# A decoder layer on one core: expert rows that carry their weight and result address, finished tiles scattered to token order, a longer tile pipeline, and blocks 0-1 and 2-3 as groups

## The chip, the cores and the metric

The kernel runs on one core of a Trainium2 chip. The metric is device time in microseconds (us) of one execution, lower is better. The chip has a tensor engine (PE, its weight loads PEld), a vector engine (DVE), a scalar engine (ACT), GpSimd (POOL) and a sync engine (SP) that in this kernel issues all plain DMAs. POOL issues the indirect ones.

## The reference

Input `x` is 2 x 1024 x 256 float32. One layer computes, on every token:

```python
x = layernorm(x + causal_linear_attention(x))          # 16 heads, 128 random features
x = layernorm(x + differential_cross_attention(ctx, x)) # 32 half-heads, 77 context rows
scores = sigmoid(x @ gate_w.T)                          # 16 experts in 4 groups
topk_idx = top 4 of the experts in the best 2 groups    # by scores + e_bias
topk_weight = 2.5 * scores[topk_idx] / sum(scores[topk_idx])
y = sum over the 4 experts of weight * (silu(x Wg) * (x Wu)) Wd   # 256 -> 128 -> 256
x = layernorm(x + y + shared_expert(x))
```

So each of the 2048 tokens has 4 expert rows, 8192 rows in all. The expert of a row is known only at run time.

## The kernel before

The tokens are cut into 4 blocks of 512 (`TB`), two for each batch element. `schedule()` writes out one list of jobs, (kind, block or group, number), and every engine walks the same list in order and does its own part of each job. An engine that waits in a job does not go on to the next one. Semaphores (`signal`) tie the parts together.

**Attention steps.** `attention_jobs(t)` gives the linear-attention work of one head per step, 64 heads' steps for 4 blocks plus 4 to drain. Jobs of the previous block's *chain* are merged between them.

**The chain of a block**, `chain_jobs(b, s)`: s=4 output projection and first norm, s=5 queries, s=7 to 9 cross-attention scores, s=10 maxima, s=11 to 15 24 `probs` chunks and 16 `weigh` jobs and the second norm, s=16 transposes, s=17 to 19 gate, routing (`route` 0 to 3 on DVE) and shared expert, and `prefix`, in which `slots(b)` makes the address of each expert row. At s=20 `dispatch` lets POOL write the rows with 16 indirect DMAs into the DRAM tensor `rows_in` of the block's group, sorted by expert, `keep` stores the residual sums, and after the last block of a group `ends` lets SP write 16 zero tiles behind the experts' last rows. In each `probs` chunk ACT makes two exponentials, and POOL subtracts (line 799) to get the low half. In each second `weigh` job POOL makes two adds (lines 804 and 808).

**Groups.** `GROUPS = ((0, 1, 2), (3,))`. The rows of a group are cut into tiles of 128 rows of one expert, worked on in pairs: 32 pairs for group 0 and 16 for group 1. `table(grp)` on DVE makes each tile's expert and first row.

**Tile steps**, `tile_jobs(grp, s)`: at step s `rows in` of pair s+2 (SP, two DMAs), `tile turn` of pair s (PE transposes, ACT high half, DVE low half), `tile up` of s-1 (12 matmuls of 256 columns on PE, tanh on ACT, two DVE products), `tile turn back` of s-2, `tile down` of s-3 (6 matmuls, ACT copies the result, line 966), and `rows out` of s-3 (SP writes the tiles to `rows_out`). The buffers `xg` and `yb` have 3 slots (`XG`).

**Order after attention.** The chain of block 2 ends, block 3's first two chain parts run, then the tile steps of group 0 with the rest of block 3's chain in their gaps: scores in steps 1 to 8, maxima in step 9, probs and weigh in steps 10 to 17, norm in step 18, transposes from step 21, `dispatch` and `ends` of block 3 in step 25. Then come the tile steps of group 1, in which POOL gathers the finished rows of blocks 0 to 2 (`gather`: 4 indirect DMAs for each 128 tokens, 12 times) and DVE combines them (`combine`: four multiply-adds, line 1359, and norm statistics) and normalizes each block (`norm3`). At the end the same is done for the 4 token tiles of block 3.

```python
for s in range(-2, PAIRS_OF[0] + 4):
    jobs += merged(tile_jobs(0, s) or [("none", 0, 0)], gaps.pop(s, []))
...
if n == 0 and b == GROUPS[GROUP_OF[b]][0]:
    ...
    for r in range(XG):
        pool.wait_ge(*yb_stored[r](len(range(r, upto_pair, XG)), 0))
```

The last lines are the wait of POOL before a group's first gather: every tile of the group must be stored.

## Time and profile before

| what | value |
|---|---|
| time of the kernel before, median of 3 | 1045.37 us (1042.42 to 1045.6) |
| profiled execution, its own time | 1054.35 us |
| its span, first to last instruction | 1052.5 us |
| mean granted TensorE clock | 0.896 |
| PE busy | 831.2 us (79%) |
| DVE busy | 670.1 us (64%) |
| ACT busy | 488.8 us (46%) |
| POOL busy | 353.2 us (34%) |

All stretches are in us from the span's start. Busy shares are an average over stages with different limits. The attention steps run to about 720, the tile steps of group 0 from about 766 to 926, those of group 1 to 1018, and the rest is the end of block 3.

### The profile page before, as it was taken

To read this page: it belongs to the slowest core of one execution; us is meant where nothing else is said; L and a number is where in the kernel's file an instruction comes from. 1 tells how busy PE (TensorE), PEld (TensorE's weight loads), DVE (VectorE), ACT (ScalarE), POOL (GpSimd) and SP (SyncE) were. 2 spreads that over 40 slices of the span, in tenths; PEclk is the share of its full clock that TensorE was granted. 3 is DMA by queue.
4 is the path that set the end of the run, shared out by engine and by line. 5 is a ranking of instruction groups with operands and counts; after the bars stand their busy time and mean duration, and the time that the engine had idled before them with its cause. 6 is when DMAs were issued, how large, how long until landed. Compare 5 with 4: busy or idle time off the path is not lost.

```text
span 1052.5 us, 19058 instructions
## 1 busy us (share of the span) xinstructions
PE 831.2 (79%) x6576; PEld 635.7 (60%) x6576; DVE 670.1 (64%) x1786; ACT 488.8 (46%) x926; POOL 353.2 (34%) x375
## 2 busy tenths in 40 slices
PE   4799978998888898889889988875278977656640
PEld 2478756866667686667667666764166765544430
DVE  5476634457556765757686576567466668749845
ACT  4667745353565425457453446610036933333320
POOL 3111101010474143048315216803202811547514
PEclk9989988999898999989999999977579988888875
DMA  7356575322121223102023321424233432757632
GB/s 279 83 146 178 138 137 143 97 71 60 41 62 40 71 86 86 31 21 52 21 71 101 81 61 31 152 80 146 64 107 115 123 93 89 240 185 237 210 106 85
DMA packets 89677, 111.04 MB, mean 105 GB/s; under 512 B 21233, under 2 KB 70513, under 8 KB 89073
## 3 DMA queue, kind: packets, MB, share of 16 engines
q1 hardware_dynamic: 83440, 93.03, 31.0%
q0 software_dynamic: 6144, 16.79, 5.1%
q8 instruction: 57, 0.93, 0.4%
q14 instruction: 36, 0.29, 0.1%
HBM read 47.58 MB, written 42.27 MB: 85 GB/s over the span
## 4 chain that ended last, share of the span: by engine, by line
PE 46%; DVE 20%; POOL 10%; issue 7%; ACT 7%; SPq 6%; DMA 3%; POOLq 0%; DVEq 0%; ACTq 0%
PE ps L1375 22%; PE ps L1472 5%; POOL prob L799 4%; POOL attn_mem L828 4%; PE ps L1475 4%; PE ps L1453 3%; SPq L635 3%; PE ps L1462 2%; PE ps L1443 1%; PE ps L1444 1%; PE ps L1445 1%; ACT square L887 1%; POOL low_parts L792 1%; DVE low_parts L1213 1%; PE ps L1432 1%
## 5 line engine op out<-in xcount | busy, mean ns | idle before, releaser
L792 POOL TENSOR_TENSOR low_parts<-square,qk 128x512 f16<-128x512 f32 x64 | 76.3, 1192 | 432.6 <-DVE qk L1215 432.6
L1375 PE MATMUL ps<-w_qkv,attn_mem 128*128 x576 | 127.5, 301 | 35.8 <-DVE attn_mem L1335 25.8
L799 POOL TENSOR_TENSOR prob<-prob_full,prob 128x512 f16<-128x512 f32 x96 | 113.8, 1211 | 65.5 <-ACT prob_full L924 64.3
L1213 DVE SCALAR_TENSOR_TENSOR low_parts<-ps,qk 128x512 f16<-128x512 f32 x64 | 44.1, 689 | 118.8 <-ACT square L887 118.8
L882 ACT ACTIVATE qk<-ps 128x512 f16<-128x512 f32 x64 | 38.2, 596 | 150.6 <-PE ps L1375 150.6
L1375 PE MATMUL ps<-x_split,w_qkv 128*128 128x512 f16 x384 | 100.2, 400 | 1.0 <-DVE low_parts L1213 1.0
L1472 PE MATMUL ps<-attn_mem 128*128 128x65 f32 x512 | 98.4, 287 | 2.9 <-issue 2.1
L814 POOL DMA_INDIRECT rows_in<-stream,slot_i x64 | 64.1, 1001 | 97.8 <-DVE slot_i L1146 79.2
L1375 PEld LDWEIGHTS ps<-w_qkv,attn_mem 128*128 128x128 f16 x576 | 61.9, 107 | 55.0 <-issue 44.8
L1472 PEld LDWEIGHTS ps<-attn_mem 128*128 128x128 f32 x512 | 85.1, 207 | 12.4 <-issue 3.5
L828 POOL DMA_INDIRECT attn_mem<-rows_out,back_i x64 | 62.1, 971 | 67.2 <-DMA rows_out<-attn_mem 48.3
L1475 PE MATMUL ps<-run,attn_mem 128*128 128x65 f32 x384 | 79.5, 291 | 0.0
L1453 PE MATMUL ps<-attn_mem 128*128 128x128 f32 x512 | 72.8, 287 | 1.2 <-issue 0.9
L1453 PEld LDWEIGHTS ps<-attn_mem 128*128 128x128 f32 x512 | 65.8, 199 | 3.1 <-issue 1.8
L898 ACT ACTIVATE attn_mem<-ps 128x512 f32<-128x512 f32 x64 | 38.3, 599 | 63.0 <-PE ps L1445 62.1
L1462 PEld LDWEIGHTS ps<-attn_mem 128*128 128x128 f32 x448 | 60.0, 196 | 12.3 <-ACT square L887 5.1
L1443 PE MATMUL ps<-qk,w_feat_high 128*128 128x512 f16 x128 | 50.6, 395 | 18.6 <-DMA qk<-low_parts 14.1
L924 ACT ACTIVATE prob_full<-ps 128x512 f32<-128x512 f32 x96 | 61.1, 639 | 7.5 <-POOL prob L799 6.4
L1475 PEld LDWEIGHTS ps<-run,attn_mem 128*128 128x128 f32 x384 | 63.5, 208 | 0.0
L1462 PE MATMUL ps<-attn_mem 128*128 128x65 f32 x448 | 59.5, 274 | 4.6 <-ACT square L887 4.2
L1375 PEld LDWEIGHTS ps<-x_split,w_qkv 128*128 128x128 f16 x384 | 39.0, 107 | 38.0 <-issue 8.8
L1375 PE MATMUL ps<-xv,prob 128*128 128x68 f16 x1152 | 47.4, 197 | 17.5 <-POOL prob L799 17.1
(242 smaller groups left out, 1983.1 us busy)
## 6 DMA issues: line engine op xcount, KB each, us to landing
qk<-low_parts SPq DMA_DIRECT2D x128, 128.0 KB, 2.3
attn_mem<-rows_in SPq DMA_DIRECT2D x96, 128.0 KB, 2.4
rows_out<-attn_mem SPq DMA_DIRECT2D x48, 256.0 KB, 2.2
late_mem<-ffn_w SPq DMA_DIRECT2D x17, 384.0 KB, 3.7
up_split<-late_mem SPq DMA_DIRECT2D x16, 256.0 KB, 3.4
rows_in<-zero_row SPq DMA_DIRECT2D x16, 256.0 KB, 2.5
rows_in<-zero_row SPq DMA_DIRECT2D x32, 128.0 KB, 2.3
xq<-late_mem SPq DMA_DIRECT2D x48, 64.0 KB, 2.0
```

The source lines that it names most:

```text
L792: pool.tensor_tensor(low_parts[:, n % 2, 1, :], square[:, n % 2, :], qk[:, n % 2, n // 2 % 2, 0, 1, :], ALU.subtract).then_inc(p_sql.sem, 1)
L799: pool.tensor_tensor(prob[:, n % RING, 1, :], prob_full[:, n % FULL, :], prob[:, n % RING, 0, :], ALU.subtract).then_inc(pr_low.sem, 1)
L814: pool.indirect_dma_start(rows_in[GROUP_OF[b]], bass.IndirectOffsetOnAxis(ap=slot_i[:, b, j:j + 1], axis=0), stream[:, b % 2, j // TOPK, : ...
L828: pool.indirect_dma_start(yg[:, i % YG, k, :], None, rows_out[GROUP_OF[b]], bass.IndirectOffsetOnAxis(ap=back_i[:, b, j:j + 1], axis=0)).t ...
L924: act.activation(prob_full[:, n % FULL, :], bank[:, :], ACT.Exp, scale=float(XD) ** -0.5).then_inc(pr_exp.sem, 1)
L1213: dve.scalar_tensor_tensor(low_parts[:, n % 2, 0, :], bank[:, :], 1 / W_SCALE, pair[:, 0, 0, :], ALU.mult, ALU.subtract).then_inc(p_low.se ...
L1375: ins = pe.matmul(dst, lhs(i), rhs(j), start=first and n == 0, stop=last and n == 2)
L1443: pe.matmul(bank[:, :], w_feat_high[:, :], source[:, 0, :], start=True, stop=False)
L1453: last = pe.matmul(bank[:, t], kf[:, n % 2, t], qf[:, n % 4, t], start=True, stop=True)
L1462: last = pe.matmul(bank[:, V1 * c:V1 * c + V1], kt[:, n % 2, c, :], v1[:, c, n, :], start=True, stop=True)
L1472: last = pe.matmul(o, att[:, (H * b + n) % 3, c, :], v1[:, c, n, :], start=True, stop=not before)
L1475: last = pe.matmul(o, qf[:, n % 4, P * c:P * c + P], held, start=False, stop=True)
```

## The change

- A row in `rows_in` has `RW` = 256 + 32 floats instead of 256: behind the token's values stand its 16 weights and 16 result addresses, one for each expert. `routing` part 3 writes them on DVE beside the values (`row_mem`). The products `wk_of`, the job `back` and its DVE work go away.
- `tile down` on ACT makes four instructions instead of one: for each tile of the pair it copies the result address (128x1) to `dest`, and copies the result (128x256) scaled with the row's weight. It reads the tiles' experts into registers once in 8 pairs.
- `rows out` (SP, one DMA for a pair) goes away. In the same job POOL now scatters each tile with an indirect DMA to `rows_out`, which is in token order, four rows for a token. `yb` has 3 slots (`YB`), and ACT waits for the scatter of three pairs before.
- `gather` (POOL, 64 indirect DMAs in all) goes away. `fetch` is one plain SP DMA of 512 KB for each 128 tokens, into 3 slots. `combine` is three DVE adds (128x512, 128x256, 128x256) instead of four multiply-adds. The store of a block is now a job `store`, two steps behind its norm in group 1.
- The tile pipeline is longer: `tile up` two steps behind `tile turn`, `turn back` four, `down` five; 8 slots for `xg`, 3 for `xgT` and `hid`. A slot of `xg` is now free after `tile down`.
- The chain is one step shorter (s=4 to 19): scores in two steps, everything behind one step earlier, the gate beside the transposes.
- `GROUPS = ((0, 1), (2, 3))`: 24 and 24 pairs instead of 32 and 16. `ends` of group 0 come with block 1's chain, in the attention steps, and the wait before group 1's first `rows in` is again for block 3's dispatch. Group 1's steps hold 8 combines and 2 norms instead of 12 and 3, and 8 combines and 2 norms follow behind them instead of 4 and 1.
- `spare` is 32 DMAs of one tile instead of 16 of two.

```diff
-GROUPS = ((0, 1, 2), (3,))
+GROUPS = ((0, 1), (2, 3))
...
-SPARE_STEP = 2
-XG = 3
 LOADED = 16
-YG = 4
+
+RW = D + 2 * NE
+
+NOWHERE = TOPK * max(TOKENS)
+NOWHERES = NE + max(SPARE)
+XG, YB, YG = 8, 3, 3
+
+UP, BACK, DOWN = 2, 4, 5
...
-    if s in (7, 8, 9):
-        jobs += several("scores", {7: range(0, 6), 8: range(6, 19), 9: range(19, 32)}[s])
-    if s == 10:
+    if s in (7, 8):
+        jobs += several("scores", {7: range(0, 14), 8: range(14, 32)}[s])
+    if s == 9:
         jobs += several("turn maxima", [0])
-    if 11 <= s <= 15:
-        for n in range(6 * (s - 11), min(6 * (s - 10), CHUNKS) + 0):
+    if 10 <= s <= 14:
+        for n in range(6 * (s - 10), min(6 * (s - 9), CHUNKS)):
             jobs += [("probs", b, n)]
             if n >= 3:
                 jobs += weighs(b, n - 3)
-        if s == 15:
+        if s == 14:
             jobs += weighs(b, CHUNKS - 1) + [("norm2", b, 0)]
+    if s == 15:
+        jobs += several("turn cross", range(2)) + several("gate", [0])
     if s == 16:
-        jobs += several("turn cross", range(2))
+        jobs += several("route", [0]) + several("shared up", range(2)) + several("route", [1])
     if s == 17:
-        jobs += several("gate", [0]) + several("route", [0]) + several("shared up", range(2)) + several("route", [1])
+        jobs += several("route", [2]) + several("shared down", range(2))
     if s == 18:
-        jobs += several("route", [2]) + several("shared down", range(2))
+        jobs += several("route", [3]) + several("prefix", [0])
     if s == 19:
-        jobs += several("route", [3]) + several("prefix", [0])
-    if s == 20:
         jobs += several("dispatch", [0]) + several("keep", [0])
         if b == GROUPS[GROUP_OF[b]][-1]:
             jobs += [("ends", GROUP_OF[b], 0)]
...
-    for kind, k in (("rows in", s + 2), ("tile turn", s), ("tile up", s - 1), ("tile turn back", s - 2),
-                    ("tile down", s - 3), ("rows out", s - 3)):
+    for kind, k in (("rows in", s + 2), ("tile turn", s), ("tile up", s - UP), ("tile turn back", s - BACK),
+                    ("tile down", s - DOWN)):
         if 0 <= k < n:
             jobs.append((kind, grp, k))
     return jobs
...
-    for s in range(4, 21):
+    for s in range(4, 20):
         chain.append(chain_jobs(b, s))
-    jobs += chain_jobs(NBLK - 2, last - H * (NBLK - 1))
+    for s in range(last - H * (NBLK - 1), 20):
+        jobs += chain_jobs(NBLK - 2, s)
     jobs += chain[0] + [("table", 0, 0)] + chain[1]
 
     gaps = {}
-    scores = [j for part in chain[2:6] for j in part]
+    scores = [j for part in chain[2:5] for j in part]
     for i in range(8):
         gaps[1 + i] = scores[4 * i:4 * i + 4]
-    gaps[9] = chain[6]
-    weigh = [j for part in chain[7:12] for j in part]
+    gaps[9] = chain[5]
+    weigh = [j for part in chain[6:11] for j in part]
     per = -(-len(weigh) // 10)
     for i in range(10):
         gaps[10 + i] = weigh[per * i:per * (i + 1)]
-    for i, part in enumerate(chain[12:]):
+    for i, part in enumerate(chain[11:]):
         gaps[21 + i] = part
-    gaps[27] = [("back", 0, 0), ("table", 1, 0), ("back", 1, 0)]
-    for s in range(-2, PAIRS_OF[0] + 4):
+    gaps[26] = [("table", 1, 0)]
+    for s in range(-2, PAIRS_OF[0] + DOWN + 1):
         jobs += merged(tile_jobs(0, s) or [("none", 0, 0)], gaps.pop(s, []))
     for s in sorted(gaps):
         jobs += gaps[s]
     first = [(bb, c) for bb in GROUPS[0] for c in range(NT)]
-    for s in range(-2, PAIRS_OF[1] + 4):
+    for s in range(-2, PAIRS_OF[1] + DOWN + 1):
         extra = []
         if 0 <= s < len(first):
-            bb, c = first[s]
-            if c == 0:
-                extra.append(("load sum", bb, 0))
-            extra.append(("gather", bb, c))
-        if 1 <= s <= len(first):
-            bb, c = first[s - 1]
+            extra.append(("fetch", *first[s]))
+        if 2 <= s < len(first) + 2:
+            bb, c = first[s - 2]
             extra.append(("combine", bb, c))
             if c == NT - 1:
                 extra.append(("norm3", bb, 0))
+        if 4 <= s < len(first) + 4 and first[s - 4][1] == NT - 1:
+            extra.append(("store", first[s - 4][0], 0))
         jobs += merged(tile_jobs(1, s) or [("none", 0, 0)], extra)
     for bb in GROUPS[-1]:
-        if bb != b:
-            jobs.append(("load sum", bb, 0))
-        for c in range(NT):
-            jobs.append(("gather", bb, c))
-        for c in range(NT):
-            jobs.append(("combine", bb, c))
-        jobs.append(("norm3", bb, 0))
+        for c in range(NT + 1):
+            if c < NT:
+                jobs.append(("fetch", bb, c))
+            if c:
+                jobs.append(("combine", bb, c - 1))
+        jobs += [("norm3", bb, 0), ("store", bb, 0)]
...
         x_split = x_split_mem[:, :].rearrange("p (r a k t) -> p r a k t", r=2, a=2, k=KD)
-        stream = sb("stream", [P, 2, NT, D])
+        row_mem = sb("rows", [P, 2, NT, RW])
+        stream = row_mem[:, :, :, 0:D]
...
-        yb = carve(attn_mem, at, XG * 2 * D).rearrange("p (r j c) -> p r j c", r=XG, j=2)
-        yg = carve(attn_mem, at, YG * TOPK * D).rearrange("p (r k c) -> p r k c", r=YG, k=TOPK)
-        sums = [x_stage[:, :, :].rearrange("p k t -> p (k t)").rearrange("p (t d) -> p t d", t=NT),
-                square[:, :, :].rearrange("p k t -> p (k t)").rearrange("p (t d) -> p t d", t=NT)]
+        yb = carve(attn_mem, at, YB * 2 * D).rearrange("p (r j c) -> p r j c", r=YB, j=2)
+        dest = sb("dest", [P, YB, 2], I32)
+        yg = [m.rearrange("p (k d) -> p k d", k=TOPK)
+              for m in (x_stage[:, :, :].rearrange("p k t -> p (k t)"), square[:, :, :].rearrange("p k t -> p (k t)"),
+                        low_parts[:, :, :, :].rearrange("p a b t -> p (a b t)").bitcast(F32))]
+        sums = [yT_stage[:, 1024 * r:1024 * r + 1024].rearrange("p (t d) -> p t d", t=NT) for r in range(2)]
...
-        rows_out = [nc.dram_tensor(f"rows_out{g}", [TILES[g] * P, D], F32, kind="Internal").ap() for g in range(NGRP)]
+        rows_in = [nc.dram_tensor(f"rows_in{g}", [ROWS[g], RW], F32, kind="Internal").ap() for g in range(NGRP)]
+        rows_out = [nc.dram_tensor(f"rows_out{g}", [NOWHERE + NOWHERES * P, D], F32, kind="Internal").ap() for g in range(NGRP)]
...
-                        sp.wait_ge(*spare_zeroed(0, sum(SPARE) // SPARE_STEP))
+                        sp.wait_ge(*spare_zeroed(0, sum(SPARE)))
...
-                        sp.wait_ge(*t_turned(0, i - XG + 1))
+                        sp.wait_ge(*t_kept(0, i - XG + 1))
...
-                elif kind == "rows out":
-                    i = pair_id(b, n)
-                    sp.wait_ge(*t_kept(0, i + 1))
-                    tiles = rows_out[b][2 * P * n:2 * P * (n + 1), :].rearrange("(j p) d -> p j d", p=P)
-                    sp.dma_start(tiles, yb[:, i % XG, :, :]).then_inc(yb_stored[i % XG].sem, 16)
-                elif kind == "load sum":
-                    if b >= 2:
-                        sp.wait_ge(*out_stored[b % 2](0, b // 2))
-                    sp.wait_ge(*sum_stored(b, 1))
-                    sp.dma_start(sums[b % 2], sum_scr[b]).then_inc(sum_loaded[b % 2].sem, 16)
-                elif kind == "norm3":
+                elif kind == "fetch":
+                    i = NT * b + n
+                    blocks = GROUPS[GROUP_OF[b]]
+                    if (b, n) == (blocks[0], 0):
+                        pairs = PAIR_BASE[GROUP_OF[b]] + len(range(PAIRS_OF[GROUP_OF[b]]))
+                        for r in range(YB):
+                            sp.wait_ge(*yb_sent[r](len(range(r, pairs, YB)), 0))
+                    if i >= YG:
+                        sp.wait_ge(*folded(0, i - YG + 1))
+                    first = TOPK * (TB * blocks.index(b) + P * n)
+                    sp.dma_start(yg[i % YG], rows_out[GROUP_OF[b]][first:first + TOPK * P, :].rearrange(
+                        "(p k) d -> p k d", k=TOPK)).then_inc(yg_loaded[i % YG].sem, 16)
+                    if n == 0 and b < NBLK - 1:
+                        if b >= 2:
+                            sp.wait_ge(*out_stored[b % 2](0, b // 2))
+                        sp.wait_ge(*sum_stored(b, 1))
+                        sp.dma_start(sums[b % 2], sum_scr[b]).then_inc(sum_loaded[b % 2].sem, 16)
+                elif kind == "store":
                     sp.wait_ge(*normed[2](b, NT))
                     done = acc[:, :, :] if b == NBLK - 1 else sums[b % 2]
...
-                elif kind == "gather":
-                    i = NT * b + n
-                    if n == 0 and b == GROUPS[GROUP_OF[b]][0]:
-                        upto_pair = PAIR_BASE[GROUP_OF[b]] + PAIRS_OF[GROUP_OF[b]]
-                        pool.wait_ge(*back_ready(0, GROUP_OF[b] + 1))
-                        for r in range(XG):
-                            pool.wait_ge(*yb_stored[r](len(range(r, upto_pair, XG)), 0))
-                    if i >= YG:
-                        pool.wait_ge(*combined(0, i - YG + 1))
-                    for k in range(TOPK):
-                        j = TOPK * n + k
+                            row_mem[:, b % 2, j // TOPK, :], None).then_inc(scattered[b].sem, 16)
+                elif kind == "tile down":
+                    i = pair_id(b, n)
+                    pool.wait_ge(*t_kept(0, i + 1))
+                    for j in range(2):
                         pool.indirect_dma_start(
-                            yg[:, i % YG, k, :], None, rows_out[GROUP_OF[b]],
-                            bass.IndirectOffsetOnAxis(ap=back_i[:, b, j:j + 1], axis=0)
-                        ).then_inc(yg_loaded[i % YG].sem, 16)
+                            rows_out[b], bass.IndirectOffsetOnAxis(ap=dest[:, i % YB, j:j + 1], axis=0),
+                            yb[:, i % YB, j, :], None).then_inc(yb_sent[i % YB].sem, 16)
 
...
                 elif kind == "tile down":
                     i = pair_id(b, n)
                     act.wait_ge(*t_down(0, i + 1))
-                    if i >= XG:
-                        act.wait_ge(*yb_stored[i % XG](i // XG, 0))
-                    act.activation(yb[:, i % XG, :, :].rearrange("p j c -> p (j c)"), bank[:, :],
-                                   ACT.Copy).then_inc(t_kept.sem, 1)
+                    if 2 * n % LOADED == 0:
+                        t = TILE_BASE[b] + 2 * n
+                        if n == 0:
+                            act.wait_ge(*table_ready(0, b + 1))
+                        experts = loaded(mybir.EngineType.Activation, expert_i[0:1, t:t + LOADED], NE - 1)
+                    if i >= YB:
+                        act.wait_ge(*yb_sent[i % YB](i // YB, 0))
+                    for j in range(2):
+                        e = experts[(2 * n + j) % LOADED]
+                        act.activation(dest[:, i % YB, j:j + 1], xg[:, i % XG, j, bass.ds(e + (D + NE), 1)], ACT.Copy)
+                        last = act.activation(yb[:, i % YB, j, :], bank[:, D * j:D * j + D], ACT.Copy,
+                                              scale=xg[:, i % XG, j, bass.ds(e + D, 1)])
+                    last.then_inc(t_kept.sem, 1)
...
-                    link(dve.tensor_tensor(weight[:, :, :], chosen[:, :, :],
+                    mark(dve.tensor_tensor(row_mem[:, b % 2, :, D:D + NE], chosen[:, :, :],
                                            w_rec2[:, :, :].to_broadcast([P, NT, NE]), ALU.mult))
+                    at_group = TOPK * TB * GROUPS[GROUP_OF[b]].index(b)
+                    mark(dve.scalar_tensor_tensor(row_mem[:, b % 2, :, D + NE:RW], e_rank[:, :, :], float(at_group),
+                                                  token_4[:, :, :].to_broadcast([P, NT, NE]), ALU.add, ALU.add))
...
-                link(dve.tensor_reduce(slot_f[:, b, :], picked.rearrange("p c k e -> p (c k) e"), AX.X, ALU.add))
-                dve.tensor_copy(slot_i[:, b, :], slot_f[:, b, :]).then_inc(slots_ready.sem, 1)
-                link(dve.tensor_tensor(picked, one_hot, weight[:, :, :].unsqueeze(2).to_broadcast(wide), ALU.mult))
-                link(dve.tensor_reduce(wk_of[:, b, :], picked.rearrange("p c k e -> p (c k) e"), AX.X, ALU.add))
+                link(dve.tensor_reduce(slot_f[:, :], picked.rearrange("p c k e -> p (c k) e"), AX.X, ALU.add))
...
-                    for k in range(TOPK):
-                        j = TOPK * n + k
-                        ins = dve.scalar_tensor_tensor(total[:, n, :], yg[:, i % YG, k, :], wk_of[:, b, j:j + 1],
-                                                       total[:, n, :], ALU.mult, ALU.add)
-                        if k < TOPK - 1:
-                            link(ins)
-                        else:
-                            ins.then_inc(combined.sem, 1)
-                            dve.wait_ge(*combined(b, n + 1))
+                    four = yg[i % YG]
+                    link(dve.tensor_tensor(four[:, 0:2, :], four[:, 0:2, :], four[:, 2:4, :], ALU.add))
+                    link(dve.tensor_tensor(four[:, 0, :], four[:, 0, :], four[:, 1, :], ALU.add))
+                    dve.tensor_tensor(total[:, n, :], four[:, 0, :], total[:, n, :], ALU.add).then_inc(folded.sem, 1)
+                    dve.wait_ge(*folded(0, i + 1))
```

The rest of the diff changes the rings' indices from 2 to 3, adds two iotas and two copies for the addresses in the setup, and removes the function `back`.

## Rows read from the trace of the kernel before

**Rows 1.** The page: chain that ended last, shares by engine.

```profile
PE 46%; DVE 20%; POOL 10%; issue 7%; ACT 7%; SPq 6%; DMA 3%; POOLq 0%; DVEq 0%; ACTq 0%
```

**Rows 2.** Windows: length, busy us (count) of PE, PEld, DVE, ACT, POOL; clock, DMA.

```profile
804.00:850.00 46.00, 41.80 (x538) 34.23 (x539) 26.47 (x64) 38.45 (x84) 34.21 (x40) 0.97 0.31 95
850.00:893.00 43.00, 30.70 (x235) 24.24 (x233) 34.15 (x98) 15.02 (x33) 1.95 (x2) 0.80 0.29 90
926.00:991.00 65.00, 36.86 (x244) 29.01 (x245) 47.69 (x129) 18.61 (x40) 46.19 (x48) 0.79 0.73 222
1018.00:1052.50 34.50, 0.00 (x0) 0.00 (x0) 13.54 (x40) 0.21 (x1) 15.25 (x16) 0.56 0.29 91
```

**Rows 3.** Timeline of 720 to 760: end of block 2's chain.

```profile
720.14 13.08 PE L1375 MATMUL ps<-w_o,yT 128*128 128x256 f16 x96 [1.40 <-DVE yT L1246]
...
723.01 0.17 DVE L1146 CAST slot_i<-slot_f 128x16 int32<-128x16 f32 x1
```

**Rows 4.** Timeline of POOL, 760 to 1053: block 3's probs and weigh.

```profile
806.07 1.15 POOL L799 TENSOR_TENSOR prob<-prob_full,prob 128x512 f16<-128x512 f32 x1 [62.20 <-ACT prob_full L924]
...
817.28 3.40 POOL L799 TENSOR_TENSOR prob<-prob_full,prob 128x512 f16<-128x512 f32 x3
821.25 0.46 POOL L804 TENSOR_TENSOR x_mem<-x_mem 128x128 f32<-128x128 f32 x1 [0.57 <-DVE x_mem L1290]
...
847.63 0.45 POOL L808 TENSOR_TENSOR stream<-stream,x_mem 128x128 f32<-128x128 f32 x1
```

**Rows 5.** The same timeline: first and last of 16 dispatches, then of 16 gathers.

```profile
890.62 0.98 POOL L814 DMA_INDIRECT rows_in<-stream,slot_i  x1 [42.54 <-DVE slot_i L1146]
...
910.74 0.97 POOL L814 DMA_INDIRECT rows_in<-stream,slot_i  x1 [0.30 <-issue]
...
1021.21 0.95 POOL L828 DMA_INDIRECT attn_mem<-rows_out,back_i  x1 [29.50 <-DMA rows_out<-attn_mem]
...
1040.07 0.96 POOL L828 DMA_INDIRECT attn_mem<-rows_out,back_i  x1 [0.30 <-issue]
```

**Rows 6.** Timeline of SP, 880 to 1053: the zero tiles and the last store.

```profile
894.97 8.36 SPq L715 DMA_DIRECT2D rows_in<-zero_row  x16
...
1049.43 0.35 SPq L749 DMA_DIRECT2D out<-acc  x1
```

**Rows 7.** Timeline of DVE, 925 to 1053: one pair, one combine, one norm.

```profile
942.00 0.66 DVE L1335 TENSOR_TENSOR attn_mem<-ps,attn_mem 128x512 f16<-128x512 f32 x1
...
943.70 2.03 DVE L1359 SCALAR_TENSOR_TENSOR x_stage<-attn_mem,wk_of,x_stage 128x256 f32<-128x256 f32 x4
...
946.33 0.66 DVE L1335 TENSOR_TENSOR attn_mem<-ps,attn_mem 128x512 f16<-128x512 f32 x1
...
955.64 0.17 DVE L1070 TENSOR_SCALAR root_v<-mv 128x4 f32<-128x4 f32 x1
...
959.36 0.68 DVE L1335 TENSOR_TENSOR attn_mem<-ps,attn_mem 128x512 f16<-128x512 f32 x1
```

**Rows 8.** Critical chain: start us, us, what.

```profile
893.15 1.65 SPq L560
...
913.31 1.31 PE ps L1375 x12
...
915.93 1.31 PE ps L1375 x12
...
1017.62 0.61 ACT attn_mem L966
```

**Rows 9.** Timeline of PE: group 1's first transposes.

```profile
931.53 2.13 PE L1594 MATMUL ps<-ident,attn_mem 128*128 128x128 f32 x8 [5.55 <-DMA attn_mem<-rows_in]
```

**Rows 10.** DMA issues: count, KB each, median us to landing.

```profile
attn_mem<-rows_in SPq DMA_DIRECT2D x96, 128.0 KB, 2.4
...
rows_in<-stream,slot_i POOLq DMA_INDIRECT x64, 2.5
...
x_stage<-sums SPq DMA_DIRECT2D x2, 512.0 KB, 6.1
...
square<-sums SPq DMA_DIRECT2D x1, 512.0 KB, 4.3
```

88 lines of the change are left out of this document (37 added, 51 removed).

## The prediction, on record before the changed kernel was seen

> **What bounds the kernel now.** The page's chain by engine comes first [rows 1]: PE holds 46% of it, DVE 20%, POOL 10%. POOL does little arithmetic, so a tenth of the chain sends the reader to the stages. The windows [rows 2] show them. While block 3's probs and weigh run among the tile steps (804 to 850), three engines are near full: PE 41.8 of 46 us, ACT 38.5, POOL 34.2. In 850 to 893, the norm and routing, DVE has 34 of 43. In 926 to 991 PE has only 37 of 65, because POOL gathers (46) and DVE combines (48). In the last 34.5 us PE does nothing. So the change acts on the last third, from 720 on. I go along the timelines of POOL, DVE, SP and PE and add up what each stretch gets longer or shorter. Before 720 little is touched.
>
> **Price of one indirect DMA.** On POOL it is 0.97 us and 0.30 us to the next, 1.27 in all: 16 gathers start 18.86 us apart from first to last, 16 dispatches 20.12 [rows 5]. It lands 2.5 us after issue [rows 10]. The change takes away 64 gathers (81 us) and adds 2 scatters for each of 48 pairs: 96, or 122 us. The rest of the argument is where these lie.
>
> **1. Up to the first tile step: -3.** Block 2's chain is one step earlier. A step is about 10.7 us (720 us over 67 steps). Today PE starts block 3's output projection at 720.14 and DVE's slot table comes at 723.01 [rows 3]. In the new order these last 3 us stand ahead of the projection, but all DVE work behind block 2's norm starts a step sooner. If DVE allows it all, the gain is 10.7 - 3 = 8; if DVE is full anyway, 0. I take -4. Against it, `ends` of group 0 (a load of registers, 1.65 us, and 8.36 us of DMA issues [rows 6, 8]) moves from a place where SP was free into attention steps, where SP moves the low halves PE waits for, and dispatch no longer coincides with the long projection step. It fits one step of slack: +1, at most +3 for each of the two blocks. `spare` in single tiles adds 16 issues over 32 steps, nothing. Two DVE products of `slots` go and one small product comes, nothing. The wider row (1152 instead of 1024 bytes) I also take as nothing.
>
> **2. Probs and weigh: +15.** POOL works from 806.07 to 848.1, 42.0 us, of which 34.2 busy; it waits 0.57 for DVE in nearly each of 8 rounds [rows 2, 4]. The 24 chunks and 16 weighs stand in gaps 10 to 17. Each of these steps now has a `tile down` with two scatters on POOL, in front of the last weigh: 16 x 1.27 = 20.3 us. In between nothing is free enough: POOL's own work of 34.2 + 20.3 = 54.5 exceeds the 42. So the stretch grows by at least 12.5 and, if no wait is absorbed, by 20.3. I take 15. Behind POOL queue the low halves, for which PE's weigh waits, and ACT's exponentials, which have three slots. ACT itself gets three more instructions a pair; bound from above by its 0.61 us copy [rows 8] that is 8 x 1.8 = 15 us on 38.5, under POOL's 54.5, so hidden; from below nothing.
>
> **3. Norm to slot table: -4.** Today 848.1 to 890.6 [rows 4, 5]. The chain runs through DVE, 34 busy of 43 [rows 2]. The gate one gap earlier and a PE that isn't held by a late product can take out part of the 9 us of idle time: between 0 and -8.
>
> **4. Slot table to the first transposes of group 1: -13.** Today it is 890.6 to 931.5, 40.9 us [rows 5, 9], because group 0 still has 7 pairs to do, and SP is blocked by `ends`. Now group 0 has only 4 pairs under way, and the path is the wait for block 3's dispatch: 21.1 us of POOL, landing 2.5, registers 1.65, rows in 0.3 + 2.4 [rows 5, 8, 10]: 28. `ends` (8.4) and group 1's table lie beside the dispatch. PE idles here, and starts at the lower clock, as it does today.
>
> **5. Group 1's tiles: +9.** Today 931.5 to 1018.2, 86.7 us for 16 pairs [rows 8, 9]. New: group 0's last four pairs scatter only behind the dispatch, 8 x 1.27 = 10.2, land in 2.5, and the first fetch with the sums behind it takes 0.5 + 6.1 [rows 10]. That is 12 us behind the first transposes, and DVE stands in the first combine till then. A pair costs DVE 1.70 and a combine 2.63 [rows 7]; four linked products of 0.51 (2.03 [rows 7]) become one add of 128x512 (about 0.7, nearest the 0.66 row) and two of about 0.5, so 2.3. Eight steps of 4.0 and two norms of 3.75 [rows 7]: 39.5. The other pairs go at PE's pace, 2.62 us [rows 8], about 16.5 of them with the filling of the longer pipeline: 43. Sum 95. Scatters take 2.54 of POOL a pair, just under 2.62, and hide; were PE faster they would bound. Bounds: 24 x 2.62 and 6 to start is 69, if the long pipeline hides all combines; 105 if fetches and DVE wait for each other.
>
> **6. The end: +6.** Today 34.3 us behind the last tile [rows 8]. New: two scatters 2.5, landing 2.5, fetch and sum 6.6, eight combines 18.4, two norms 7.5, last store 3.1 (1049.43 to 1052.5 [rows 6]): 40.6. Fetches keep up only if 512 KB come every 2.3 us, 228 GB/s; 926 to 991 moved 222 [rows 2]. Bounds: +3 with the 4.3 us row [rows 10], +12 if a fetch takes 3 us.
>
> The Trainium skill, DMA: Bandwidth & Descriptors, section Anatomy of one DMA, gives 2.0 us plus the bytes over 436 GB/s. By it a fetch alone would be an estimated 3.2 us instead of the row's 6.1, and terms 5 and 6 would be 3 less each.
>
> **Sum.** -3 + 15 - 4 - 13 + 9 + 6 = +10, from a span of 1052.5 to about 1062. The profiled execution's own time is 1054.35, the median shown 1045.37, 9 less; I apply the difference to the median: 1055.4, given as 1055.
>
> **Rivals.**
> - *The long pipeline pays.* UP, BACK and DOWN let PE run ahead through DVE's combines and norms. For it: today PE stands idle 28 of 65 us beside gathers and combines [rows 2], and the gathers' order is gone. Against it: every engine keeps its order, and DVE has 4.0 us of work in these steps. It decides if group 1 takes under 85 us. With term 5 at -5, term 3 at -8 and term 2 at 12.5, the sum is -10: 1035.
> - *A draw.* POOL's 13 to 15 us in term 2 and the 13 us regained in term 4 cancel, and 5 and 6 come out at +3 together with 3 at -6: within 3 us, 1045.
> - *POOL becomes the engine of the whole tile phase.* `yb` has three slots; ACT, in order, waits for the scatter of three pairs before, and with it exponentials and turns. While POOL does the 21 us dispatch no scatter goes. If ACT and POOL wait for each other in term 2, it is +20 or more, term 5 is at 105, term 6 at +10: together +28, 1073.
> - *The descriptor lock.* If DVE's adds, now with two inputs in SBUF, hold up POOL's scatters, each costs more beside a combine. Gathers today run beside combines with two such inputs, 48 in the window at 46.19 / 48 = 0.96 us [rows 2], so it isn't seen; 16 scatters at double price would add at most 20 us, 1075. The Trainium skill, SBUF - State Buffer, section Who interferes with whom, says that a two-input DVE instruction contends with what GpSimd reads, and copies in a two-port mode with both; the trace shows no such delay of gathers.
>
> **Chances and range.** Forecast 0.50, long pipeline 0.22, draw 0.10, POOL or lock 0.18 (lock 0.03). About 0.3%, 3 us, is what a measurement of this kernel can tell from no change. The forecast lies above it nearly always, and some of its 0.50 goes to neither side: faster 0.25, same 0.10, slower 0.65. The forecast's own range, from the bounds of terms 2, 5 and 6, is 1049 to 1066. Over all cases it reaches from 1033 to 1076.
>
> **What the changed profile should show.** POOL busy with hardly a pause from the first prob to the last weigh, that stretch 55 to 60 us. Block 3's dispatch about 8 us later than 890.6. PE idle for over 10 us before group 1, its first transposes near 926. DVE waiting for the first fetch, then steps of 4 us. The last tile near 1022, and about 40 us behind it. Wrong would be: probs and weigh in under 50 us, steps beside a combine at under 3.5 us, or a tail of under 36.

## The result, and the profile after

| | median, us | runs |
|---|---|---|
| before | 1045.48 | 4 (1042.42 to 1050.55) |
| changed | 1067.47 | 4 (1062.01 to 1080.78) |

The ratio is 1.0188, with a 95% interval from 1.0112 to 1.0264. It leaves out the changed kernel's longest run, 1080.78, as one of the slow state; by it the change costs 20 us, by the medians of all runs 22. I had forecast 10 (1055, range 1033 to 1076). The profiled execution of the changed kernel is its longest, 1080.78 us with a span of 1079.0, against 1062 to 1071 for the others. A later profile, of a kernel that differs only behind block 3's first fetches (a5_store_later below, span 1069.5), shows the same stretches from block 3's first prob to the last tile within 0.4 us each, so these can be read.

The chain by engine, which answers to [rows 1]; POOL's share has grown, not fallen:

```profile
PE 45%; DVE 23%; POOL 12%; issue 7%; SPq 5%; ACT 5%; DMA 3%; ACTq 0%; POOLq 0%; DVEq 0%
```

Windows of the changed kernel, columns as in [rows 2]: block 3's probs and weigh; norm and routing; dispatch; group 1's tiles; the tail.

```profile
808.00:869.00 61.00, 43.93 (x533) 36.35 (x534) 23.98 (x61) 42.30 (x109) 49.77 (x56) 0.92 0.24 75
869.00:907.00 38.00, 26.10 (x219) 21.17 (x217) 31.33 (x91) 15.91 (x49) 13.53 (x14) 0.87 0.21 69
908.00:935.00 27.00, 3.73 (x22) 2.39 (x23) 8.12 (x22) 4.59 (x18) 20.60 (x22) 0.61 0.65 215
935.00:1031.00 96.00, 74.89 (x576) 61.40 (x574) 65.75 (x168) 50.74 (x160) 43.51 (x45) 0.88 0.59 196
1031.00:1079.00 48.00, 0.00 (x0) 0.00 (x0) 23.21 (x72) 2.16 (x8) 5.81 (x6) 0.53 0.39 140
```

In the first window POOL has 49.8 of 61 us; PE and ACT have about 43. In the third nearly everything stands still. In the last PE does nothing for 48 us.

Put end to end, the two profiles differ by 26.5 us (1079.0 against 1052.5):

| stretch | before | changed | difference | forecast |
|---|---|---|---|---|
| 1. start to block 3's first prob | 806.1 | 807.9 | +1.8 | -3 |
| 2. first prob to last weigh addition | 42.0 | 60.6 | +18.6 | +15 |
| 3. to the dispatch | 42.5 | 39.4 | -3.1 | -4 |
| 4. to group 1's first transposes | 40.9 | 26.6 | -14.3 | -13 |
| 5. to the last tile's copy on ACT | 86.7 | 98.8 | +12.1 | +9 |
| 6. to the end | 34.3 | 45.7 | +11.4 | +6 |

**Term 2 in the trace.** POOL's timeline (start, duration, line) of one round of three chunks and two tiles, which answers to [rows 4]:

```profile
822.40 0.99 POOL L836 DMA_INDIRECT rows_out<-attn_mem,dest  x1 [0.16 <-issue]
823.69 0.97 POOL L836 DMA_INDIRECT rows_out<-attn_mem,dest  x1 [0.30 <-issue]
824.69 2.26 POOL L814 TENSOR_TENSOR prob<-prob_full,prob 128x512 f16<-128x512 f32 x2
826.91 0.45 POOL L819 TENSOR_TENSOR x_mem<-x_mem 128x128 f32<-128x128 f32 x1
827.44 0.46 POOL L823 TENSOR_TENSOR rows<-rows,x_mem 128x128 f32<-128x128 f32 x1
827.86 1.16 POOL L814 TENSOR_TENSOR prob<-prob_full,prob 128x512 f16<-128x512 f32 x1
829.17 0.99 POOL L836 DMA_INDIRECT rows_out<-attn_mem,dest  x1 [0.16 <-issue]
```

From 822.40 to 829.17 is 6.77 us, and no gap in it is a wait for another engine: a full POOL. Before, the five rounds from 817.28 [rows 4] to the first row below took 4.79 us each, and four of them held a wait of 0.57. So a full round costs 2.0 us more, 16 us over eight rounds. Towards the end of the stretch POOL is not full: it waits 3.55 us for ACT before the stretch's last pair (second row below), where the longest wait of before was 1.58.

```profile
841.22 3.39 POOL L799 TENSOR_TENSOR prob<-prob_full,prob 128x512 f16<-128x512 f32 x3
```

```profile
865.24 0.99 POOL L836 DMA_INDIRECT rows_out<-attn_mem,dest  x1 [3.55 <-ACT attn_mem L981]
```

**Terms 4 to 6.** SP's zero tiles and the first rows of group 1 (first fence), two DVE steps beside a combine (second), POOL's last eight pairs (third), ACT's two waits for a `yb` slot (fourth), then SP and DVE in the tail (fifth, sixth). The fences are timelines of the engine named in each row.

```profile
909.64 10.32 SPq L721 DMA_DIRECT2D rows_in<-zero_row  x16
930.98 0.90 SPq L740 DMA_DIRECT2D attn_mem<-rows_in  x2
```

```profile
953.75 0.66 DVE L1337 TENSOR_TENSOR attn_mem<-ps,attn_mem 128x512 f16<-128x512 f32 x1
955.45 0.68 DVE L1360 TENSOR_TENSOR low_parts<-low_parts 128x512 f32<-128x512 f32 x1
...
957.64 0.66 DVE L1337 TENSOR_TENSOR attn_mem<-ps,attn_mem 128x512 f16<-128x512 f32 x1
```

```profile
1018.29 0.97 POOL L836 DMA_INDIRECT rows_out<-attn_mem,dest  x1 [1.36 <-ACT attn_mem L981]
1019.56 0.97 POOL L836 DMA_INDIRECT rows_out<-attn_mem,dest  x1 [0.30 <-issue]
...
1037.38 0.97 POOL L836 DMA_INDIRECT rows_out<-attn_mem,dest  x1 [0.31 <-issue]
```

```profile
932.20 0.20 ACT L980 ACTIVATE dest<-attn_mem 128x1 int32 x1 [20.26 <-DMA rows_out<-attn_mem,dest]
...
1031.13 0.20 ACT L980 ACTIVATE dest<-attn_mem 128x1 int32 x1 [1.93 <-DMA rows_out<-attn_mem,dest]
```

```profile
1057.53 0.34 SPq L762 DMA_DIRECT2D out<-yT  x1
1057.92 0.42 SPq L752 DMA_DIRECT2D x_stage<-rows_out  x1
```

```profile
1056.11 1.38 DVE L1100 TENSOR_SCALAR yT<-yT,mv,rstd 128x256 f32<-128x256 f32 x4
1062.90 0.69 DVE L1360 TENSOR_TENSOR x_stage<-x_stage 128x512 f32<-128x512 f32 x1 [5.41 <-DMA x_stage<-rows_out]
```

A step beside a combine takes 3.89 us. From 1018.29 on the 16 scatters of the last eight pairs follow each other at 1.27 us: PE drains the pipeline faster than POOL sends, ACT waits 1.93 us for one of the three `yb` slots, and POOL ends 5.0 us behind ACT's last copy (1033.4). With the short pipeline (a2_short_pipe below) it is still 4.4 us behind, so the backlog is hardly a matter of the pipeline's length. ACT's longer wait, 20.26 us, lies under the dispatch, during which no scatter goes; it ends 2.4 us ahead of group 1's first transposes, for which ACT then waits 2.5 us, so no cost of it is seen. In the tail SP waits with the store of block 2 for its norm, and behind that store in the queue stands block 3's first fetch: DVE waits 5.41 us for it.

### The profile page after: what moved, and what is told of

It is laid out like the page before. It is cut to its first block, busy times and chain, and to the rows that moved or that the text cites. A ratio compares the mean times of both kernels' runs of the same rounds, so it can differ in the third digit from the quotient of the medians.

```text
span 1079.0 us, 19374 instructions
## 1 busy us (share of the span) xinstructions
PE 834.6 (77%) x6576; PEld 636.5 (59%) x6576; DVE 656.5 (61%) x1756; ACT 509.1 (47%) x1070; POOL 383.2 (36%) x409
## 4 chain that ended last, share of the span: by engine, by line
PE 45%; DVE 23%; POOL 12%; issue 7%; SPq 5%; ACT 5%; DMA 3%; ACTq 0%; POOLq 0%; DVEq 0%
PE ps L1373 20%; POOL prob L814 6%; PE ps L1470 4%; PE ps L1473 4%; PE ps L1451 3%; POOL rows_out L836 3%; PE ps L1460 3%; SPq L641 3%; PE ps L1441 2%; PE ps L1443 2%; PE ps L1442 2%; POOL rows_in L829 1%; PE ps L1430 1%; POOL low_parts L807 1%; DVE xmax L1272 1%
## 5 line engine op out<-in xcount | busy, mean ns | idle before, releaser
L1373 PE MATMUL ps<-w_qkv,attn_mem 128*128 x576 | 122.0, 292 | 33.7 <-DVE attn_mem L1351 29.6
L836 POOL DMA_INDIRECT rows_out<-attn_mem,dest x96 | 93.3, 972 | 137.7 <-ACT attn_mem L981 117.8
L829 POOL DMA_INDIRECT rows_in<-rows,slot_i x64 | 62.4, 976 | 56.4 <-DVE slot_i L1167 37.8
L1337 DVE TENSOR_TENSOR attn_mem<-ps,attn_mem 128x512 f16<-128x512 f32 x48 | 32.9, 686 | 77.0 <-ACT attn_mem L954 76.7
L1373 PE MATMUL ps<-xv,prob 128*128 128x68 f16 x1152 | 49.7, 200 | 36.1 <-POOL prob L814 34.4
L1373 PEld LDWEIGHTS ps<-xv,prob 128*128 128x128 f16 x1152 | 46.7, 102 | 47.2 <-issue 30.9
L1460 PEld LDWEIGHTS ps<-attn_mem 128*128 128x128 f32 x448 | 61.4, 201 | 10.6 <-ACT square L894 2.8
```

The costliest lines, as they stand in the source:

```text
L829: pool.indirect_dma_start(rows_in[GROUP_OF[b]], bass.IndirectOffsetOnAxis(ap=slot_i[:, b, j:j + 1], axis=0), row_mem[:, b % 2, j // TOPK, ...
L836: pool.indirect_dma_start(rows_out[b], bass.IndirectOffsetOnAxis(ap=dest[:, i % YB, j:j + 1], axis=0), yb[:, i % YB, j, :], None).then_inc ...
L1373: ins = pe.matmul(dst, lhs(i), rhs(j), start=first and n == 0, stop=last and n == 2)
L1460: last = pe.matmul(bank[:, V1 * c:V1 * c + V1], kt[:, n % 2, c, :], v1[:, c, n, :], start=True, stop=True)
```

## The experiments

They ran in three sets. In each, the kernel before ran among them: its median was 1120.56 us in the first, 1046.94 in the second and 1122.70 in the third. The first two sets were on the same chip. Ratios are to the kernel before of the same set, with the 95% interval; a variant is compared with the changed kernel in its own set where that ran. Why the level moved is the last section's matter.

**a0_same and d0_after: the changed kernel again.** No edit.

> The changed kernel, unchanged, once more. Both theories: the time lies within 0.5% of the 1067.47 us median of its first runs. It gives a profile to read the others against: from the first prob's low half on POOL to the last weigh's addition 57 to 61 us, steps beside a combine 3.9 us, and the last tile's scatter to the end of the span 40 to 42 us.

> The changed kernel, unchanged, as the mark for the other three and for the three variants of the call before. My theory: the ratio to the kernel before is that of the first comparison, 1.019 to 1.026 (1066 to 1074 us where before takes 1047), and the 1.0016 of one session came from that session's slow SP. The rival: the changed kernel is really within 1% of before and the first comparison was off; then the variants with 1.025 are slower than it.

Measured 1122.12 us, ratio 1.0016 (0.9986 to 1.0046), in the first set, and 1126.35, 1.0043 (1.0014 to 1.0072), in the third. The first expectation failed in the absolute time, the second in the ratio: the cost of the change, 20 to 22 us at first, was 2 to 5 us under these conditions. The stretches of the tail and of the probs were in place (probs 63.8 and 63.7 us, longer than the 57 to 61 expected; last matmul to the end 46.5 and 50.4), so neither shrank; the kernel before lost more elsewhere.

**c0_before: the kernel before, for a profile of its own.** No edit.

> The kernel before, unchanged, for a profile on the chip on which the experiments run. On that chip the two kernels took the same time (1120.6 and 1122.1 us), where the first chip had 22 us between them. My reading: SP's instructions take about 0.39 us each there beside POOL's indirect DMAs, against 0.21 on the first chip, and the kernel before loses more by it since its gathers lie beside the tiles: group 1's tiles (first transposes to the last matmul) take 100 us or more instead of 86, and everything up to block 3's probs and the probs themselves (42 us) lie as on the first chip but for a lower clock. The rival: the difference is only the granted clock; then group 1's tiles take 86 to 92 us, and the whole difference lies ahead of 720 us.

Measured 1048.82 us, 1.0013 (0.9979 to 1.0048), in the second set, which turned out to be like the first comparison. Group 1's tiles, first transposes to the last matmul, took 87.5 us and the probs 42.0, against 86 and 42.0 in the first profile of before. It confirms that profile, and tells nothing between my reading and the rival, since the conditions of the first set were gone.

**a1_groups_back and d1_groups_back: the groups as they were.**

```diff
-GROUPS = ((0, 1), (2, 3))
+GROUPS = ((0, 1, 2), (3,))
```

> The changed kernel with its groups as they were, blocks 0 to 2 and block 3; everything else stays. Theory one (the groups cost the time: terms 5 and 6 fall due to group 1 having the combines of two blocks before its tiles end and two blocks behind them): only four fetches and combines and one norm lie behind the last tile, so the stretch behind it is about 27 us instead of 41, and the 7 pairs of group 0 that are left cover block 3's dispatch and the wait for its rows; the time falls by 20 us or more, to 1047 or less. Theory two (POOL's 96 scatters cost the time wherever they stand): 12 combines and three norms now lie beside 16 tile steps, DVE is full there and POOL's scatters stay, so that what the tail gives, the tile steps take back; the time stays within 5 us of the changed kernel.

> The changed kernel with its groups as they were, once more. It was 13 us faster than the changed kernel in a session in which SP's issues beside the dispatch took 26 us. If that wait was what it had left to gain (PE idle for 26 us behind the slot table), it is now 20 to 28 us faster than the changed kernel, about the time of before. If POOL's scatters bound it instead, it stays at 10 to 15 us faster, and over before by 0.7% or more.

Measured 1108.58 us, 0.9897 (0.9853 to 0.9942), and 1113.74, 0.9897 (0.9854 to 0.9940): 13.5 and 12.6 us faster than the changed kernel beside it, and 1% faster than before. Windows of d1_groups_back: dispatch to group 1, group 1's 16 pairs, tail.

```profile
941.00:1002.00 61.00, 26.25 (x201) 21.65 (x202) 21.18 (x54) 18.95 (x64) 33.72 (x35) 0.76 0.44 149
1002.00:1089.00 87.00, 55.72 (x387) 44.22 (x385) 62.42 (x172) 35.78 (x115) 32.53 (x33) 0.81 0.59 203
1089.00:1116.60 27.60, 0.00 (x0) 0.00 (x0) 11.61 (x36) 1.05 (x4) 4.83 (x5) 0.50 0.34 124
```

The tail is 27.6 us instead of 46.5 and 50.4 (last matmul to the end), as theory one had it. Group 1's tiles, now 16 pairs instead of 24, take 87 us instead of the 104.6 of a0_same. But the gain of 20 us or more in the time is too high: the stretch from the dispatch to group 1, 38.6 and 40.9 us in the changed kernel of these sets, is 61 here: 12 pairs of group 0 end in it instead of 4, and PE stands idle for 27.7 us of it behind SP's zero transfers. So the two-block group costs some 13 us net, in terms 5 and 6. It was not run in the second set, in which SP was quick, so d1_groups_back's question stays open.

**a8_aside: 16 scatters fewer among the probs.** For 8 pairs SP sends the tiles to an unused tensor with plain transfers; their results are missing from the output. Not shown are the added stores that fill the missing rows with zeros in the attention stage, and the waits that follow from the edit.

```diff
-                elif kind == "tile down":
+                elif kind == "tile down" and not (b == 0 and 5 <= n < 13):
...
+                elif kind == "tile down" and b == 0 and 5 <= n < 13:
...
+                    sp.wait_ge(*t_kept(0, i + 1))
+                    for j in range(2):
+                        sp.dma_start(aside[(2 * n + j) * P:(2 * n + j + 1) * P, :], yb[:, i % YB, j, :]
```

> The changed kernel, in which the 8 pairs whose last step stands among block 3's probs and weighings are not scattered by POOL: SP stores each of their tiles with one plain transfer to an unused tensor (their 16 tiles of results are missing from the output, and the scattered rows are set to zero once in the attention stage). Theory one (POOL sets the pace of that stretch): 16 scatters by 1.27, 20.3 us, leave POOL; the stretch from the first prob to the last weigh falls from about 60 to 44 to 47 us, and the whole by 12 to 16 us. Theory two (ScalarE's three more instructions a pair, and the wait for one of the three slots, hold the stretch; POOL is busy beside it): the stretch stays above 54 us and the whole falls by under 6 us.

Measured 1104.43 us, 0.9861 (0.9820 to 0.9902): 17.7 us faster than a0_same. Windows of probs and weigh, a0_same first, then a8_aside:

```profile
838.00:902.00 64.00, 45.98 (x529) 37.60 (x530) 33.73 (x60) 41.22 (x108) 49.97 (x56) 0.87 0.23 71
```

```profile
829.00:874.00 45.00, 38.98 (x511) 31.80 (x511) 21.34 (x57) 38.74 (x102) 33.66 (x40) 0.97 0.31 92
```

The stretch falls from 63.8 to 45.7 us, inside 44 to 47, although ACT still has its extra copies. The whole falls by more than the 12 to 16 us expected. Theory one holds: the scatters of this stretch cost about all that they take on POOL, 16 x 1.27 less 2.

**a7_low_on_dve: another way to relieve POOL.** Every second low half of block 3 moves to DVE; the first two lines make POOL skip them.

```diff
+                    if low_on_dve(b, n):
+                        continue
...
+                elif kind == "probs" and low_on_dve(b, n):
+                    dve.wait_ge(*pr_exp(b, n + 1))
+                    dve.tensor_tensor(prob[:, n % RING, 1, :], prob_full[:, n % FULL, :], prob[:, n % RING, 0, :],
+                                      ALU.subtract).then_inc(pr_low_dve.sem, 1)
```

> The changed kernel with every second low half of block 3's probs made by DVE instead of POOL: 12 instructions of 1.22 us leave POOL, about 0.7 us each go to DVE. Theory one (POOL alone sets the pace, 6.76 us a round of three chunks, with no waits): POOL falls to about 36 us of work in the stretch, ScalarE's 43.6 us is next, and the stretch from first prob to last weigh goes from about 61 to 47 to 52 us; the whole is 9 to 14 us faster. Theory two (POOL and ScalarE hold each other up through the three slots of results): the stretch stays above 56 us, the whole gains under 4 us.

Measured 1076.87 us, 1.0254 (1.0199 to 1.0309): no gain that can be told, where 9 to 14 us were expected (the changed kernel wasn't in this set). POOL did fall to 40.0 us of work, but the stretch only from 60.6 to 56.4. DVE's lines there (count, busy us, mean ns), then DVE's and POOL's timelines at one place:

```profile
L1303 DVE TENSOR_TENSOR prob<-prob_full,prob 128x512 f16<-128x512 f32 x12 | 14.3, 1199 | 5.3 <-ACT prob_full L946 5.2
L1310 DVE TENSOR_TENSOR xrec<-xrec,coef 128x16 f32<-128x16 f32 x8 | 7.1, 891 | 0.3
```

```profile
846.18 1.67 DVE L1310 TENSOR_TENSOR xrec<-xrec,coef 128x16 f32<-128x16 f32 x1
...
851.95 0.18 DVE L1310 TENSOR_TENSOR xrec<-xrec,coef 128x16 f32<-128x16 f32 x1
```

```profile
846.64 1.17 POOL L829 TENSOR_TENSOR prob<-prob_full,prob 128x512 f16<-128x512 f32 x1
```

The same tiny DVE product of 128x16 takes 0.18 us alone and 1.67 when POOL's low half runs; it ends at 847.85, POOL's at 847.81. The moved low halves take 0.69 at best and 1.20 in the mean. The stretch above 56 us is what theory two forecast, but not for its reason: POOL was relieved, and DVE became the one that was held up, 42.6 busy of 57 us. The Trainium skill, SBUF — State Buffer, section Who interferes with whom, has it that a DVE instruction with two inputs in SBUF contends with a GpSimd instruction that reads SBUF; this trace agrees.

**a2_short_pipe: the short pipeline.**

```diff
-UP, BACK, DOWN = 2, 4, 5
+UP, BACK, DOWN = 1, 2, 3
```

> The changed kernel with the pipeline as short as before (up, turn back and down 1, 2 and 3 steps behind the turn). My theory (every engine keeps its order, so the long pipeline brings nothing beside combines and only adds two steps of filling and draining per group): 0 to 6 us faster than the changed kernel. The rival that the long pipeline pays (PE runs ahead of DVE's combines, of ScalarE and of POOL): 8 us slower or more, most of it beside combines and in the stretch of block 3's probs.

Measured 1076.24 us, 1.0264 (1.0205 to 1.0323). The changed kernel wasn't in this set; against its 1.0188 (to 1.0264) of the first comparison and the 1.025 of the two others of the set, nothing is gained in the time. Its window of group 1's tiles:

```profile
933.00:1025.00 92.00, 72.43 (x576) 60.69 (x576) 65.81 (x168) 51.50 (x164) 42.56 (x43) 0.91 0.61 204
```

92 us instead of the changed kernel's 96, with the same DVE work. The probs took 61.4 and the tail 47.0. The long pipeline doesn't pay beside combines; it costs 4 us there.

**d2_groups_short: groups as they were and the short pipeline**, both edits above.

> Groups as they were and the short pipeline (1, 2 and 3 steps), the scatters to token order stay. If the long pipeline only costs filling and draining, 2 to 5 us faster than the one with the groups alone; if it pays beside combines (12 of them now lie beside 8 pairs), slower by 5 us or more.

Measured 1113.26 us, 0.9932 (0.9897 to 0.9967), 0.5 us under d1_groups_back by the medians and 0.35% over it by the ratios: no difference that can be told. Neither sign of the expectation is borne out.

**a5_store_later: the store of block 2 behind block 3's first three fetches.**

```diff
-        jobs += [("norm3", bb, 0), ("store", bb, 0)]
+            if c == 2:
+                tail += held
...
+        held = [("store", bb, 0)]
```

> The changed kernel with one job moved: SP's store of block 2's result stands behind block 3's first three fetches, not before them. In the tail of the profile SP waits for the norm in front of that store, and DVE then waits 5.4 us for block 3's first fetch. Theory one (the store's place is what makes DVE wait): the wait of 5.4 us goes, the tail is 40 us instead of 45 from the last scatter on, and the whole is 4 to 6 us faster. Theory two (the fetches are bound by the memory that they read, 512 KB in 5 us, whichever place they have): DVE waits as long for each later fetch, and the whole is within 2 us.

Measured 1072.52 us, 1.0246 (1.0196 to 1.0296). DVE's timeline at the place of the wait:

```profile
1052.08 1.38 DVE L1106 TENSOR_SCALAR yT<-yT,mv,rstd 128x256 f32<-128x256 f32 x4
1053.37 0.68 DVE L1366 TENSOR_TENSOR x_stage<-x_stage 128x512 f32<-128x512 f32 x1
```

The wait is gone. ACT's last copy to the end takes 40.3 us instead of 45.7: 5.4, the whole wait. Theory two is refuted by the profile. In the time it can't be seen by itself, since the changed kernel wasn't in the set: 3.7 and 4.4 us under the medians of the other two variants, whose intervals overlap its own. With the 5.4 us put back, the changed kernel would have taken about 1078 us in this set, an estimate from the profile's wait: 31 us over before (26 to 36 by the interval of this run), above the 12 to 28 of the first comparison's interval or at its upper end. By the same estimate a2_short_pipe and a7_low_on_dve could each have gained 1 to 2 us.

**b1_chain: the chain drawn together, alone, on the kernel before.**

```diff
-    if s in (7, 8, 9):
-        jobs += several("scores", {7: range(0, 6), 8: range(6, 19), 9: range(19, 32)}[s])
+    if s in (7, 8):
+        jobs += several("scores", {7: range(0, 14), 8: range(14, 32)}[s])
...
```

> The kernel before with one part of the change, the chain of a block drawn together by one step (scores in two steps, the gate beside the turn of the cross attention's result), and the step of block 3's chain that follows from it. My term 1 and 3 (the chain alone gains 4 us at block 2 and some of the 4 us between the last weighing and the slot table): faster by 4 to 8 us. The rival (DVE is full in the attention stage, so a step given back is no time): within 2 us of before.

Measured 1118.80 us, 0.9963 (0.9933 to 0.9993): faster by 4 us (0.8 to 7.5). The median lies at the lower end of the 4 to 8 us expected of terms 1 and 3 together. The interval reaches into the 2 us of the rival, so it is not ruled out.

**d3_groups_ends4: the zero transfers of `ends` in four lots.**

```diff
+    for q in range(1, 4):
+        gaps.setdefault(25 + q, []).append(("ends", NGRP - 1, q))
...
-                    for r in loaded(mybir.EngineType.SP, end_i[0:1, b, :], ROWS[b] - P):
+                    for r in loaded(mybir.EngineType.SP, end_i[0:1, b, NE // 4 * n:NE // 4 * (n + 1)], ROWS[b] - P):
```

> Groups as they were, and the 16 zero transfers behind the last dispatch are issued in four lots of four between the transfers of four pairs' rows, instead of in one piece. One piece takes SP 8 to 10 us where rows are issued two steps, 5.2 us, ahead of PE: if SP's place in line is what PE waits for behind the slot table, PE's wait there shrinks by 3 to 6 us and the whole with it, and the kernel is at or below the time of before. If the wait is for something else, no change against the groups alone.

Measured 1112.38 us, 0.9897 (0.9867 to 0.9927). Its window that answers to the first of d1_groups_back:

```profile
946.00:1003.00 57.00, 32.11 (x208) 24.00 (x208) 21.19 (x53) 19.84 (x68) 34.07 (x35) 0.73 0.48 161
```

PE's single wait of 27.7 us is gone and the stretch is 4.7 us shorter, but the time is 1.4 us under that of d1_groups_back and the ratio the same, less than can be told. POOL has 34 us of work in both windows, DVE 21. No gain is seen from ending what PE waited for; which engine sets the end there was not settled.

## Why the prediction was right, and where its sizes were off

The sign was right, and so was the mechanism of terms 2 and 4 to 6, though the store in the tail was left out; terms 1 and 3 were not tested by themselves. The size was half. Against the profiled spans, 26.5 against 10, term by term:

1. *Up to the first tile step.* +1.8 instead of -3, and +7.3 between the profiles of c0_before and a5_store_later, which does the changed kernel's work up to there. The drawn chain alone gives the whole kernel 4 us (b1_chain), which is what terms 1 and 3 share. What takes them back is not shown: block 3's output projection began 7.3 us later, but in the third set d0_after reaches its first prob 8 us ahead of b1_chain's in the first. The profiles of one kernel differ by more than this term ahead of 740.
2. *Probs and weigh.* +18.6 instead of +15, inside 12.5 to 20.3. I took a value between "all waits absorbed" and "none"; in sum it came out near "none", and a8_aside gives back the same 18. I had misread the waits of 0.57: they stood in four of the eight rounds. In the full rounds they were absorbed (6.76 us instead of 4.79, 16 us in eight). The other 3 us lie at the ends of the stretch, with the new wait of 3.55 for ACT; why ACT comes late there is not shown.
3. *Norm to slot table.* -3.1 for -4.
4. *To group 1.* -14.3 for -13. Most of PE's time there is idle, 15.5 us in one piece.
5. *Group 1's tiles.* +12.1 for +9 (the sum as written, 94.5 less 86.7, gives 8). The step beside a combine, 3.89 us for 4.0, and the combine, 2.2 for 2.3, were right. DVE could start the first combine 10.3 us behind the first transposes, for 12; the eight steps and two norms took 39.6 (944.95 to 984.59), for 39.5; the pairs behind them took 48.8, for 43, and that is the part that was mis-sized. "Scatters take 2.54 of POOL a pair, just under 2.62, and hide; were PE faster they would bound" is where it gave way: in the drain PE was faster, and POOL bound the last eight pairs. How much of the 48.8 that is was not separated; with the short pipeline the stretch was 93.9 us instead of 98.8.
6. *The end.* +11.4 for +6, and this is the largest miss. The working left out the store: 5.4 us of wait, shown by a5_store_later. POOL's backlog adds 2.5 (5.0 us behind the last copy instead of 2.5). The eight combines at 2.2 and the landing were a little cheaper than taken. A fetch with the sums took 5.0 us from issue to use, less than the 6.6 of the sum. The 3.2 us estimated by the Trainium skill's DMA: Bandwidth & Descriptors, section Anatomy of one DMA, was too low for it; the page gives its formula for transfers issued by GpSimd, and this one was issued by SP.

The range of the forecast, 1049 to 1066, does not follow from the bounds it names: added up, the bounds of terms 2, 5 and 6 give 1023 to 1076.

The rivals. *The long pipeline pays*: refuted, the short one is 4 us shorter in group 1. *POOL becomes the engine of the whole tile phase*: true of two stretches, the probs and the drain, not of the middle (43.5 of 96 us); ACT waited for a `yb` slot twice, 20.26 us under the dispatch, where it cost nothing that is seen, and 1.93 in the drain. *The descriptor lock*: refuted for scatters, 0.972 us in the mean over 96; but DVE and POOL do hold each other up where both are arithmetic with two inputs in SBUF (a7_low_on_dve). *A draw*: near to it in the first and third set (1.0016 and 1.0043), for another reason than the one given.

The net of the experiments: 16 scatters among the probs 18 us, the two-block last group 13 net, the store 5. No version was both free of these and tried beside before when before took 1047 us; with the groups as they were the changed kernel beat before by 1% (0.9897, twice) when before took 1121.

## What to carry to other kernels

When work is added to an engine that is near full, take nearly the full price: 20 us of scatters put 18.6 on a stretch in which POOL had 8 idle. When the tail is summed up, walk each queue in order, stores too: a store in front of a fetch makes the fetch wait for what the store waits for. And an engine that keeps up at the steady pace of a pipeline may bound its drain; the last group is best the smallest, since all behind it stands bare.

## What the runs showed of the hardware

The same kernel on the same chip took 1120.6 us in one set and 1046.9 in the next. The mean granted clock was lower too, 0.871 against 0.899 in the median of its runs, but that explains little: PE's busy time is 845 us in a0_same against 835 in the first profile of the same kernel, 11 of the 52 us between their spans. What the traces show is that the time is lost from POOL's first indirect DMA on. At that place (368.5 us in the first profile) a0_same is 3.5 us behind and d0_after 1.4, at block 3's first prob 30.5 and 24.8, at the end 51.8 and 53.1. While POOL issues, the other engines stall again and again. Block 3's output projection on PE under the dispatch of block 2 took 13.4 us in the first profile (first fence); in d0_after its first 11.6 us ran as fast, then it came in pieces and ended at 764.4, 23.2 us behind its start (three of the pieces, second fence):

```profile
727.46 13.44 PE L1373 MATMUL ps<-w_o,yT 128*128 128x256 f16 x96 [2.70 <-DVE yT L1250]
```

```profile
741.18 11.55 PE L1373 MATMUL ps<-w_o,yT 128*128 128x256 f16 x79 [2.70 <-DVE yT L1250]
753.38 0.38 PE L1373 MATMUL ps<-w_o,yT 128*128 128x256 f16 x2 [0.65 <-issue]
...
757.63 1.10 PE L1373 MATMUL ps<-w_o,yT 128*128 128x256 f16 x3 [1.62 <-issue]
```

POOL's own indirect DMAs keep their price, 0.97 us. SP's 16 zero transfers beside the dispatch took 10.3 us in the first profile, and in a0_same:

```profile
942.79 31.44 SPq L721 DMA_DIRECT2D rows_in<-zero_row  x16
```

b1_chain has its gathers beside the tiles. Its window of group 1, and ACT's timeline inside it, in which POOL gathered without a pause:

```profile
977.00:1088.00 111.00, 63.86 (x384) 47.78 (x384) 67.78 (x184) 28.52 (x63) 44.99 (x47) 0.70 0.49 153
```

```profile
984.85 0.38 ACT L954 ACTIVATE attn_mem<-ps 128x256 f32<-128x256 f32 x1 [4.30 <-PE ps L1376]
989.80 0.60 ACT L948 ACTIVATE attn_mem<-ps 128x512 f16<-128x512 f32 x1 [4.57 <-remote]
1003.15 0.38 ACT L954 ACTIVATE attn_mem<-ps 128x256 f32<-128x256 f32 x1 [12.75 <-remote]
```

ACT waits 12.75 us for something that the profile does not name ("remote"). No such wait stands in the first profiles or in c0_before; a0_same has them on ACT and DVE from 384 us on, behind the first dispatch. In this kernel group 1's tiles, first transposes to the last matmul, take 111 us against 86 of before in the first comparison; in a0_same, without gathers, 104.6 against 96.1. That difference of 17 us is about what the change's cost shrank by. It supports my reading that the old design suffers more when the other engines are slow beside indirect DMAs; but the old kernel itself was not profiled under these conditions (c0_before was meant for that), and what slowed the engines in the first and third set was not found. In this kernel the chain is drawn together too, which the comparison takes as nothing.
